# A Mamba layer between two FFNs on one core: a new order of steps, and the convolution's history added by GpSimd behind the taps

## What is computed

```python
x = x + 0.5 * ffn(layernorm(x))                 # FFN 0
x = x + mamba(layernorm(x))                     # mamba has its own norm and residual
x = x + 0.5 * ffn(layernorm(x))                 # FFN 1

# ffn
xr = mu_r * x + (1 - mu_r) * x_prev;  xk = mu_k * x + (1 - mu_k) * x_prev
out = sigmoid(xr @ W_r.T) * (square(relu(xk @ W_k.T)) @ W_v.T)

# mamba, 1024 inner features, 16 states
xs, z = split(xn @ W_in.T)
xc = silu(b_conv + sum(xp[:, k:k+L] * W_conv[:, k] for k in range(4)))   # xp: xs behind 3 zeros
dt_low, B, C = split(xc @ W_xproj.T)
delta = softplus(dt_low @ W_dt.T + b_dt)
h_t = exp(delta * A) * h_(t-1) + delta * B * xc;   y_t = sum_n h_t * C_t
out = ((y + D_skip * xc) * silu(z)) @ W_out.T + residual
```

## Time and profile before

| | |
|---|---|
| median of 3 runs | 5024.93 us (5024.33 to 5025.49) |
| profiled execution | 5020.26 us, its span 5017.6 us |
| VectorE busy | 4519.5 us (90%) |
| TensorE busy | 4273.2 us (85%) |
| GpSimd busy | 3130.9 us (62%) |
| ScalarE busy | 2904.2 us (58%) |

### The profile page before, as it was taken

The page is one execution under the profiler, slowest core; times in us unless marked ns, Lnnn a source line. Parts: engine busy times, 40 slices in busy tenths (PEclk is TensorE's granted clock), DMA queues, the critical chain, the costliest instruction groups (busy, mean ns, idle before and its releaser), DMA issues.

```text
span 5017.6 us, 57715 instructions
## 1 busy us (share of the span) xinstructions
PE 4273.2 (85%) x16640; PEld 2413.0 (48%) x16640; DVE 4519.5 (90%) x3778; ACT 2904.2 (58%) x6355; POOL 3130.9 (62%) x3200
## 2 busy tenths in 40 slices
PE   6678889898898979889898888979889898889777
PEld 2344545454554545445454454545445454554443
DVE  2799999999999999999999999999999999999982
ACT  3556656566665666656566665666656565665552
POOL 1656667576675757667575675756667575675761
PEclk9888999999999999999999999999999999999789
DMA  1546555565655656556565665656566565654651
GB/s 63 160 130 186 160 163 183 148 185 152 188 168 153 178 151 191 163 163 189 142 184 151 186 171 152 178 154 188 167 167 184 144 187 144 185 168 140 174 157 63
DMA packets 423053, 810.69 MB, mean 162 GB/s; under 512 B 41265, under 2 KB 41265, under 8 KB 418641
## 3 DMA queue, kind: packets, MB, share of 16 engines
q1 hardware_dynamic: 422736, 807.00, 56.0%
HBM read 772.25 MB, written 34.60 MB: 161 GB/s over the span
## 4 chain that ended last, share of the span: by engine, by line
PE 41%; DVE 30%; issue 14%; ACT 7%; POOL 5%; DMA 3%; DVEq 0%; SPq 0%; POOLq 0%; ACTq 0%
DVE decay L1037 13%; PE y_acc L500 9%; PE mm L416 9%; DVE g L1045 7%; PE mm L427 6%; PE mm L405 4%; PE mm L442 4%; DVE xc L997 4%; POOL dbx L1252 3%; PE mm L452 3%; PE mm L464 2%; DMA c_all<-bc_scratch 2%; PE mm L476 2%; ACT L788 1%; ACT L780 1%
## 5 line engine op out<-in xcount | busy, mean ns | idle before, releaser
L1252 POOL TENSOR_TENSOR dbx<-u,b_all 128x1024 f32<-128x1024 f32 x1024 | 2412.5, 2356 | 1475.4 <-DVE g L1045 1472.4
L1037 DVE TENSOR_TENSOR_SCAN decay<-decay,state,dbx 128x1024 f32<-128x1024 f32 x1024 | 2406.9, 2351 | 196.0 <-ACT decay L832 191.0
L500 PE MATMUL y_acc<-ident,g 128*128 128x128 f32 x8192 | 1169.2, 289 | 494.4 <-DVE g L1045 465.7
L500 PEld LDWEIGHTS y_acc<-ident,g 128*128 128x128 f32 x8192 | 994.3, 148 | 1029.8 <-DVE g L1045 724.7
L1045 DVE TENSOR_TENSOR g<-decay,c_all 128x1024 f32<-128x1024 f32 x1024 | 1244.4, 1215 | 12.2 <-issue 1.0
L829 ACT ACTIVATE decay<-delta,neg_a 128x512 f32<-128x512 f32 x1024 | 708.6, 692 | 37.7
L832 ACT ACTIVATE decay<-delta,neg_a 128x511 f32<-128x511 f32 x1024 | 686.6, 671 | 0.0
L427 PE MATMUL mm<-wbuf_c,col 128*128 128x512 f32 x1024 | 460.7, 593 | 7.8 <-ACT delta L780 7.0
L838 ACT ACTIVATE state<-decay 128x2 f32<-128x2 f32 x1024 | 168.4, 164 | 506.0 <-DVE g L1045 504.0
L997 DVE SCALAR_TENSOR_TENSOR xc<-mm,conv_sb,xc 128x509 f32<-128x509 f32 (+2 forms) x384 | 287.5, 749 | 13.6
L427 PEld LDWEIGHTS mm<-wbuf_c,col 128*128 128x128 f32 x1024 | 185.1, 190 | 198.5 <-issue 196.9
(11 more groups left out here) (98 smaller groups left out, 5379.0 us busy)
## 6 DMA issues: line engine op xcount, KB each, us to landing
b_all<-bc_scratch SPq DMA_DIRECT2D x1024, 256.0 KB, 3.9
c_all<-bc_scratch SPq DMA_DIRECT2D x1024, 256.0 KB, 4.7
wbuf_d<-in_w_r SPq DMA_DIRECT2D x32, 1024.0 KB, 8.0
wbuf_c<-in_w_v SPq DMA_DIRECT2D x32, 1024.0 KB, 8.2
xin<-in_x SPq DMA_DIRECT2D x16, 1024.0 KB, 5.4
wbuf_c<-in_w_k SPq DMA_DIRECT2D x16, 1024.0 KB, 8.5
wbuf_d<-in_w_in SPq DMA_DIRECT2D x16, 1024.0 KB, 8.1
wbuf_a<-in_w_in SPq DMA_DIRECT2D x16, 1024.0 KB, 9.6
```

What stands on the lines that cost most here:

```text
L500: last = pe.matmul(y_acc[:, tb, j * P:(j + 1) * P], g[:, s % PAIRS, j, tb * P:(tb + 1) * P], ident[:, :], start=n == 0 and j == 0 and tb % ...
L1037: dve.tensor_tensor_scan(d, d, flat(dbx[:, s % DBX, :, :]), state[:, batch, s, 0:1], ALU.mult, ALU.add).then_inc(scan_done, 1)
L1252: pool.tensor_tensor(dbx[:, s % DBX, :, :], u[:, q % 2, :, :], b_all[:, s % BRING, :].unsqueeze(1).broadcast_to([P, QT, W]), ALU.mult).the ...
```

## The change

Two things. First, `conv_taps` no longer adds `head`; the new `add_head` on GpSimd adds it behind the taps (it waits for c2), three steps after the step of the taps, and `conv_tanh` waits for that instead of for c2. Second, a new order of steps for TensorE, ScalarE, VectorE, GpSimd and the DMA issues: in FFN 1 the r groups come before the k groups; the work of steps 28 to 63 is laid out anew; the last gate goes from step 0 of the next iteration to step 63; some mixes of FFN 0 shift by a step; several weight loads and the load of x are issued earlier or later.

```diff
-                  ("f1k0", -1, f_act[1], "rel0", 1), ("xs6", 1, m_dve, "c2_6", 0),
-                  ("f1k1", -1, f_act[1], "rel1", 1), ("xs7", 1, m_dve, "c2_7", 0),
-                  ("f1k2", -1, f_act[1], "rel2", 1), ("f1k3", -1, f_act[1], "rel3", 0),
-                  ("xp", 1, m_act, "xp", 1), ("f1r0", -1, f_act[1], "th0", 0),
...
+                  ("f1r0", -1, f_act[1], "th0", 1), ("f1r1", -1, f_act[1], "th1", 1),
+                  ("xs6", 1, m_dve, "c2_6", 0), ("f1r2", -1, f_act[1], "th2", 1),
+                  ("f1r3", -1, f_act[1], "th3", 1), ("xs7", 1, m_dve, "c2_7", 0),
+                  ("f1k0", -1, f_act[1], "rel0", 1), ("f1k1", -1, f_act[1], "rel1", 0),
+                  ("xp", 1, m_act, "xp", 1), ("f1k2", -1, f_act[1], "rel2", 0),
+                  ("f1k3", -1, f_act[1], "rel3", 1), ("dt0_0", 1, h_act, "xa0", 0),
...
 # SP: the step at which each is issued
-                    if back and s == 1:      # w_out, second half
+                    if back and s == 0:
-                    if front and s == 29:    # residual to DRAM
+                    if front and s == 28:
-                    if scn and s == 46:      # w_out, first half
+                    if scn and s == 48:
-                    if scn and s == 48:      # w_in, last quarter
+                    if scn and s == 54:
-                    if front and s == 51:    # B and C to DRAM
+                    if front and s == 52:
-                    if ahead and s == 54:    # x
+                    if ahead and s == 47:
-                    if ahead and s == 55:    # w_r
+                    if ahead and s == 47:
-                    if ahead and s == 61:    # w_k
+                    if ahead and s == 59:
 # TensorE
-                    if front and s in (28, 30, 34, 36, 38, 40, 42, 44):      # xs
+                    if front and s in (28, 30, 34, 36, 38, 40, 43, 46):
-                    if back and s in (41, 43, 45, 46):                       # ffn_k
-                    if front and s in (47, 48):                              # xproj
-                    if scn and s == 49:                                      # sum_skip 3
-                    if back and 50 <= s < 54:                                # ffn_r
-                    if scn and s == 54:                                      # z 4
-                    if back and s in (55, 57, 58, 59):                       # ffn_v
-                    if front and s == 56:                                    # dt_proj 0
-                    if scn and s in (60, 61):                                # z 5, 6
+                    if back and s in (41, 42, 44, 45):                       # ffn_r
+                    if back and s in (47, 48, 51, 52):                       # ffn_k
+                    if front and s in (49, 50):                              # xproj
+                    if scn and s == 51:                                      # sum_skip 3
+                    if front and s == 53:                                    # dt_proj 0
+                    if back and 54 <= s < 58:                                # ffn_v
+                    if scn and 58 <= s < 61:                                 # z 4, 5, 6
 # ScalarE
-                act.wait_ge(m_dve.sem, m_dve.at(k, f"c2_{e}"))
+                act.wait_ge(m_pool.sem, m_pool.at(k, f"head{e}"))
-                    make_res at 28, ffn_norm(1) at 32, skip_columns(3) at 35
+                    make_res at 27, ffn_norm(1) at 30, skip_columns(3) at 41
-                    if front and s in (30, 32, 36, 38, 40, 42, 44, 46):      # conv_tanh
+                    if front and s in (30, 32, 37, 38, 40, 42, 45, 48):
-                    x_rows at 50, softplus 0 at 57, ffn_norm(0) at 63
+                    x_rows at 51, softplus 0 at 54, ffn_norm(0) at 58
 # VectorE
-                dve.wait_ge(m_pool.sem, m_pool.at(k, "h4"))
-                dve.tensor_tensor(xc2[:, e, 0:HIST], xc2[:, e, 0:HIST], head[:, e, :],
-                                  ALU.add).then_inc(m_dve.sem, 1)
-                dve.wait_ge(m_dve.sem, m_dve.at(k, f"head{e}"))
-                    if front and s in (29, 31, 35, 37, 39, 41, 43, 45):      # conv_taps
-                    if front and s in (33, 34, 36, 38, 40, 42, 44, 46):      # conv_silu
+                    if front and s in (29, 31, 35, 37, 39, 41, 44, 47):
+                    if front and s in (33, 34, 40, 42, 43, 45, 48):          # tile 7 at 48 too
-                    ffn_mix_k(1) at 38, 39; ffn_mix_r(1) at 40, 41; ffn_gate(1) at 56, 58, 59, 60
+                    ffn_mix_r(1) at 38, 40; ffn_mix_k(1) at 42, 43, 45, 46; ffn_gate(1) at 55 to 58
-                    row_stats(0) two each at 58, 59; row_means at 60
+                    row_stats(0) one each at 51 to 54; row_means at 55
-                    gate_silu at 0, 28, 30, 33, 38, 55, 61, 62
+                    gate_silu at 28, 30, 33, 38, 59, 60, 61, 63
 # GpSimd
+            def add_head(k, e):
+                pool.wait_ge(m_dve.sem, m_dve.at(k, f"c2_{e}"))
+                pool.tensor_tensor(xc2[:, e, 0:HIST], xc2[:, e, 0:HIST], head[:, e, :],
+                                   ALU.add).then_inc(m_pool.sem, 1)
+                    if front and s in (32, 34, 38, 40, 42, 44, 47, 50):
+                        add_head(f, (32, 34, 38, 40, 42, 44, 47, 50).index(s))
-                    make_u(f, 0) at 61; ffn_add(1) at 60, 62, 63, 63; ffn_rstd(0) at 63
+                    make_u(f, 0) at 57; ffn_add(1) at 59 to 62; ffn_rstd(0) at 58
```

More of the change, by code:

```diff
@@ L137, in build @@
         newton = ["guess"] + [f"{q}{i}" for i in range(NEWTON) for q in ("yy", "vyy", "half", "y")]
[L138 to L142, removed]
+        f_pe = [Marks(sem("ffn0_pe"), "T0 T1 T2 T3 k0 k1 k2 k3 r0 r1 r2 r3 v0 v1 v2 v3"),
+                Marks(sem("ffn1_pe"), "T0 T1 T2 T3 r0 r1 r2 r3 k0 k1 k2 k3 v0 v1 v2 v3")]
+        f_act = [Marks(sem("ffn0_act"), "ln0 ln1 ln2 ln3 xn0 xn1 xn2 xn3 lead last pk0 pk1 pk2 pk3 "
+                       "pr0 pr1 pr2 pr3 rel0 sq0 rel1 sq1 rel2 sq2 rel3 sq3 th0 th1 th2 th3"),
+                 Marks(sem("ffn1_act"), "ln0 ln1 ln2 ln3 xn0 xn1 xn2 xn3 lead last pr0 pr1 pr2 pr3 "
+                       "pk0 pk1 pk2 pk3 th0 th1 th2 th3 rel0 sq0 rel1 sq1 rel2 sq2 rel3 sq3")]
+        f_dve = [Marks(sem("ffn0_dve"), "st0 st1 st2 st3 mv0 mv1 mv2 mv3 xk0 xk1 xk2 xk3 xr0 xr1 xr2 xr3 "
+                       "g0 g1 g2 g3"),
+                 Marks(sem("ffn1_dve"), "st0 st1 st2 st3 mv0 mv1 mv2 mv3 xr0 xr1 xr2 xr3 xk0 xk1 xk2 xk3 "
+                       "g0 g1 g2 g3")]
         f_pool = [Marks(sem(f"ffn{i}_pool"), ["v"] + newton + ["mean", "shift", "o0", "o1", "o2", "o3"])
@@ L894, in body @@
                         mamba_columns(f, 2 * (s - 26) + 1, other)
-                    if front and s == 28:
+                    if front and s == 27:
                         make_res(f)
+                    if back and s == 30:
+                        ffn_norm(1, b, front)
+                    if scn and s in (28, 30):
+                        gate_tanh(it, s // 2 - 14)
+                    if front and s in (29, 31, 35, 37, 39, 41, 44, 47):
+                        conv_start(f, (29, 31, 35, 37, 39, 41, 44, 47).index(s), fb)
                     if scn and s == 29:
                         skip_columns(it, 2)
-                    if scn and s in (28, 30):
-                        gate_tanh(it, s // 2 - 14)
-                    if front and s in (29, 31, 35, 37, 39, 41, 43, 45):
-                        conv_start(f, (29, 31, 35, 37, 39, 41, 43, 45).index(s), fb)
-                    if back and s == 32:
-                        ffn_norm(1, b, front)
                     if scn and s in (33, 38):
@@ L940, in body @@
                         lead_decay(f, 0)
-                    if front and s == 59:
+                    if front and s == 56:
                         skip_columns(f, 0)
-                    if scn and s in (61, 62):
-                        gate_tanh(it, s - 56)
-                    if ahead and s == 63:
+                    if ahead and s == 58:
                         ffn_norm(0, it + 2)
+                    if scn and s in (59, 60, 61, 63):
+                        gate_tanh(it, (59, 60, 61, 63).index(s) + 4)
             run(body, act)
@@ L1061, in body @@
                         gate_y(b, 7)
-                    if front and s in (4, 5):
-                        ffn_mix_k(0, f, 2 * (s - 4))
-                        ffn_mix_k(0, f, 2 * (s - 4) + 1)
+                    if front and s in (3, 4, 5):
+                        ffn_mix_k(0, f, s - 3)
+                    if front and s == 5:
+                        ffn_mix_k(0, f, 3)
                     if back and s in (6, 21, 23, 25):
                         out_add(b, (6, 21, 23, 25).index(s))
[L1067 to L1071, removed]
+                    if front and s in (6, 7, 8):
+                        ffn_mix_r(0, f, (0, 1, 3)[s - 6], xn_col[:, other, :, :])
+                    if front and s == 7:
```

(15 more changed lines are left out.)

118 lines of the change are left out of this document (56 added, 62 removed).

## The result

The changed kernel takes 5075.16 us (4 runs, 5074.52 to 5076.31) against 5024.63 us before, ratio 1.0102, 95% interval 1.0084 to 1.0119. The forecast was 4979, range 4885 to 5045: the time moved the other way, and beyond the range.

A forecast was written before the change was run, and what follows sets the result against it. VectorE was taken to bound the kernel, busy 4519.5 of 5017.6 us. Per chunk 3.7 + 1.0 - 0.8 - 1.0 = 2.9, taken as 3.0; with fill and drain 46 us together, giving 4979, range 4885 to 5045.

The forecast's parts named there:

- The history add: Adding head on GpSimd instead of VectorE gains up to 3.7 us a chunk; 1.6 if long adds had another reason.
- GpSimd's add blocks nothing: GpSimd's wait for the taps costs no product: cost 0, at most 2.4 us a chunk if one were late.
- Steps 28 to 35: ffn_norm moves to step 30 before the gate's tanh; small waits eat 1.4 us that the first history add gives up.
- Gate 1 waits 0.8: At step 30, gate 1 waits 0.8 us with ffn_norm ahead of its tanh; scan(31) waits another 0.4.
- transfers only for steps 47 and 48: Loads of x, w_r and w_out, 3 MB within three steps, costed at 0; a late c row adds 2 to 3 us.
- Steps 49 to 55: keep_y behind k1 delays xproj, x_rows and scan(52); stalls of 5.9 us a chunk against 4.7 before.
- The slower rival: TensorE runs slowly after idling for keep_y, costing 5 to 6 us a chunk; 5062 us, chance 0.17.
- Front part: Steps 0 to 27: last gate moves to step 63, some mixes shift; gain 0.7 us a chunk.
- Fill and drain: Start and end of the run: 2 to 3 us won in the fill, 1 to 2 us lost in the drain.
- The new order as a whole: All moved steps without the history add: stalls of 17.5 us a chunk against 16.5, so 1.0 lost.
- Its own signs: Wrong if a chunk is under 295 or over 300.4 us, scan(49)-scan(55) under 26 or over 31, or c rows delay VectorE.

The follow-up runs named there:

- the repaired order: Changed kernel with both waits removed: ffn_norm of FFN 1 at step 32, keep_y(2) ahead of k1's activations in step 49; 4939.27 us, ratio 0.9838.
- experiment 7: Kernel before, old order, with the history add still on VectorE but behind the taps; 5021.78 us, ratio 1.0004.
- experiments 3 and 9: 3: kernel before, only the history add moved to GpSimd, 4977.43 us. 9: the repaired order with the history add back on VectorE, 4994.71 us.
- experiment 1: Changed kernel with ffn_norm of FFN 1 moved back from step 30 to step 32 on ScalarE; 4999.22 us, ratio 0.9948.

## Why the prediction was wrong

- **The history add: right.** Forecast 3.7 us a chunk, up to 15 or 16 x 3.7 = 55 to 59 us; measured alone in the old order 46, in the repaired order 55. That the long adds end with GpSimd's product is borne out by all 214 long adds (experiment 7), but no run took GpSimd's product away from an add and left the rest, so the mechanism is seen in the rows, not isolated. The Trainium skill (GPSIMD Engine Reference, section 1, Specifications) names the shared SBUF interface; the rows agree, 1.58 us for three columns. The Trainium skill's advice on elementwise work (the same page, section 4.1, Engine selection), which the prediction weighed against the change, did not decide: 128 adds took GpSimd 210 ns each in the changed kernel, 26.9 us.
- **GpSimd's add blocks nothing: right** in its cost. ScalarE does wait 68.1 us for it in the changed kernel, yet with both waits removed it is 24.6, no more than the 24.8 us that it waited for the taps before, and the add gains in experiments 3 and 9.
- **Steps 28 to 35: this step failed.** "Gate 1 waits 0.8": I priced ffn_norm at step 30 by its own 2.91 us and gave no term to the residual store that it waits for, which put that wait at nothing without a reason. The gate waits 4.36 us and scan(31) 0.24, 4.6 for the 1.2 of the sum. With the old landing time, 6.8 us, the store would have landed at 2703.4, before ScalarE came to ffn_norm at 2704.15. But the store's own move, one step earlier, put it right behind two 1 MB loads, and 6.8 us became 11.4. The prediction counted transfers only for steps 47 and 48, where nothing came of them (c rows ended 0.9 us of VectorE's waits in all). Repairing it at ScalarE is worth 76 us, at the DMA queue 62.
- **Steps 49 to 55: right mechanism, mis-sized.** The chain was the one that the sum followed, keep_y behind k1, TensorE idle, xproj, x_rows, scan(52). It gave 2.3, 0.8, 1.2, 1.7 us; measured 4.16, 0.99, 1.13, 1.68. The first term lacked the lower clock after TensorE's idle time: 1.61 us for the sum where 1.09 is usual and 4.73 for the group where it is 3.65, 1.6 us together, and 0.3 around them. The slower rival had named this, at 5 to 6 us a chunk and for three groups; it was the sum with one group, and some 1.9 us. By itself it would not have cancelled the gain, as experiment 1 shows, where it stands and the time is 0.5% under before.
- **Front part: mis-sized.** From scan(0) to scan(11) the changed kernel takes 47.7 us in the median chunk where it took 48.4, the last gate's move out of step 0 included. One of the moved mixes met a product that was late behind make_u, 1.2 us that the sum did not have.
- **Fill and drain: near.** Forecast 2 to 3 us won and 1 to 2 lost. The first scan starts at 155.03 us instead of 156.66, 1.6 won, and from the start of the last scan to the end it takes 109.2 instead of 107.5, 1.7 lost.
- **The new order as a whole** was forecast to lose 1.0 - 0.2 = 0.8 to 1 us a chunk in stalls; it lost 58 us, 3.6 a chunk.
- **Its own signs.** A chunk over 300.4 us (303.76) and scan(49) to scan(55) over 31 us (31.40, 28.9 by the sum) both came, VectorE's busy time fell by 34.6 us and not by about 50, and the wait for `xs_last` hardly shrank.

## What to carry to other kernels

When an operation is moved up in an in-order engine, look for every semaphore that it waits for, and price the one that is a DMA by what is issued ahead of it in the new order, not by its old landing time. Two changes in one diff can have opposite signs: here the small one gained 46 us and the big one lost 58. And a wait that another engine needs (keep_y, 1.07 us) belongs in front of work that nobody waits for at once.

## What the runs showed of the hardware

- A VectorE operation of three columns with both inputs in SBUF took 1.58 us where it takes 0.16, ending with GpSimd's running 128x1024 product (2683.50 and 2683.49 us). All 214 adds over 0.25 us in four traces end so. A 128x512 mix took 1.95 us in such a place.
- A 1 MB store issued 2.2 us behind one 1 MB load and 5.2 us behind another landed in 11.4 us in the median, in 6.8 where they stood 9.7 and 12.7 us ahead, and in 6.6 with those loads behind it.
- After 2.42 us of idle time TensorE's granted clock was 0.61 of full speed in the sum that followed and 0.76 in the next group, which took 4.73 us. Without that idle time it was 1.00 and the same group took 3.65.
